# Scan convolutions as diagonal matmuls, 64-row steps in two row tiles, and doubled buffers, in a four-stage image kernel

## The reference

```
L0: channel attention: q,k,v = 1x1 convs; softmax over 64 channels; per image
L1: deformable 3x3 conv: offsets and mask = conv3x3(x); bilinear samples of x
    at 9 taps x mask; sum_k w_dcn[:, :, k] @ sample_k; batch norm; relu
L2: spatial attention: softmax(q^T k / 8) over 256 pixels; x + proj(attn @ v)
L3: y = depthwise3x3(ln2d(x));  o = sum over 4 directions of
    conv1d_5(y) * sigmoid(G_d y + g_b);  x = x + fuse(o)
    z = ff1(ln2d(x)); a, g = split(z); x + ff2(a * sigmoid(g))
```

## Time and profile before

| What | Value |
|---|---|
| median of the runs | 418.3 us (414.33 to 418.74) |
| span of the profiled execution | 416.3 us; its own run time is not listed apart, and it lies inside the runs |
| PE busy | 355.3 us (85%), 2060 matmul records |
| DVE busy | 286.1 us (69%) |
| ACT busy | 205.2 us (49%) |
| POOL busy | 107.6 us (26%) |
| chain that ended last | PE 52%, DVE 29%, issue 9%, ACT 6% |

### The profile page before, as it was taken

The page is one execution under the profiler, slowest core; times in us unless marked ns, Lnnn a source line. Parts: engine busy times, 40 slices in busy tenths (PEclk is TensorE's granted clock), DMA queues, the critical chain, the costliest instruction groups (busy, mean ns, idle before and its releaser), DMA issues.

```text
span 416.3 us, 6350 instructions
## 1 busy us (share of the span) xinstructions
PE 355.3 (85%) x2060; PEld 192.6 (46%) x2060; DVE 286.1 (69%) x623; ACT 205.2 (49%) x463; POOL 107.6 (26%) x178
## 2 busy tenths in 40 slices
PE   3759989998899989999899989999899988944613
PEld 2643545645455553645464554555464434324301
DVE  2226535595965878496978697596858698877681
ACT  1163365367416672477537652576337653543512
POOL 0130220140413231330424140422223141142241
PEclk9979999999869996899999986999689999997655
DMA  7000000000000000000000000000000000000000
GB/s 236 14 0 2 14 2 2 13 2 0 2 1 2 1 28 0 2 1 25 0 0 0 27 0 0 0 0 25 0 0 0 13 1 0 2 13 0 0 13 13
DMA packets 3042, 4.66 MB, mean 11 GB/s; under 512 B 336, under 2 KB 2768, under 8 KB 2896
## 3 DMA queue, kind: packets, MB, share of 16 engines
q1 hardware_dynamic: 3024, 4.43, 3.3%
HBM read 3.38 MB, written 1.05 MB: 11 GB/s over the span
## 4 chain that ended last, share of the span: by engine, by line
PE 52%; DVE 29%; issue 9%; ACT 6%; POOL 1%; DMA 1%; DVEq 0%; ACTq 0%; SPq 0%; POOLq 0%
PE ps_cv L497 13%; DVE sb_acc L992 10%; DVE sb_wt L933 5%; DVE sb_dw_acc L978 5%; PE ps_yb L481 5%; PE ps_ma L421 5%; PE ps_mb L568 4%; PE ps_mb L542 3%; PE ps_xb L478 3%; PE ps_mb L528 3%; PE ps_wx L465 2%; PE ps_mc L590 2%; ACT sb_xe L717 2%; PE ps_ma L412 2%; PE ps_ma L450 2%
## 5 line engine op out<-in xcount | busy, mean ns | idle before, releaser
L933 DVE TENSOR_TENSOR sb_wt<-ps_yb,sb_xe 128x512 f32<-128x512 f32 x144 | 97.2, 685 | 65.4 <-ACT sb_xe L717 49.2
L497 PE MATMUL ps_cv<-sb_wt,sb_w_x 128*64 128x256 f32 x576 | 100.0, 428 | 0.0
L481 PE MATMUL ps_yb<-sb_hats,sb_sel 128*128 128x512 f16 x144 | 57.6, 409 | 3.9 <-DVE sb_wt L933 3.7
L497 PEld LDWEIGHTS ps_cv<-sb_wt,sb_w_x 128*64 128x64 f32 x576 | 29.8, 141 | 55.3 <-issue 49.8
L992 DVE SCALAR_TENSOR_TENSOR sb_acc<-sb_y_pad,sb_par,sb_acc 128x256 f32<-128x256 f32 x96 | 52.1, 596 | 2.5 <-ACT sb_acc L788 2.4
L717 ACT ACTIVATE sb_xe<-ps_xb 128x512 f32<-128x512 f32 x72 | 43.0, 597 | 9.4 <-PE ps_xb L478 9.4
L1115 POOL TENSOR_TENSOR sb_acc<-sb_acc,sb_g_tmp 128x256 f32<-128x256 f32 x32 | 24.9, 779 | 63.2 <-ACT sb_acc L788 59.6
L978 DVE SCALAR_TENSOR_TENSOR sb_dw_acc<-sb_z_pad,sb_par,sb_dw_acc 128x256 f32<-128x256 f32 x56 | 36.7, 704 | 3.2 <-ACT sb_dw_acc L773 3.1
L465 PE MATMUL ps_wx<-sb_par,sb_x 128*128 128x256 f32 (+1 forms) x144 | 36.6, 376 | 0.4 <-ACT sb_w_x L708 0.4
L1075 POOL TENSOR_TENSOR sb_dist<-sb_pos,sb_par 128x1152 f32<-128x1152 f32 (+1 forms) x8 | 16.7, 2089 | 71.4 <-DVE sb_pos L886 71.4
L743 ACT ACTIVATE sb_b_exp<-ps_mb,sb_b_neg 128x256 f32<-128x256 f32 x28 | 13.0, 470 | 41.7 <-DVE sb_b_neg L943 41.7
(11 more groups left out here) (172 smaller groups left out, 547.4 us busy)
## 6 DMA issues: line engine op xcount, KB each, us to landing
sb_par<-in_par SPq DMA_DIRECT2D x1, 1339.5 KB, 8.5
sb_x_in<-in_x SPq DMA_DIRECT2D x8, 128.0 KB, 2.1
out_y<-sb_y_out SPq DMA_DIRECT2D x8, 128.0 KB, 1.7
sb_par<-in_par SPq DMA_DIRECT2D x1, 397.0 KB, 4.6
sb_sel<-in_sel SPq DMA_DIRECT2D x1, 224.0 KB, 4.7
sb_par<-in_par SPq DMA_DIRECT2D x1, 192.0 KB, 2.7
sb_par<-in_par SPq DMA_DIRECT2D x1, 128.0 KB, 2.2
```

Of the source, the lines that this page charges most:

```text
L481: nc.tensor.matmul(yb[h][:, :], sel_sb[:, P * (3 + 2 * odd + h):P * (4 + 2 * odd + h)], hats[:, g, :], start=True, stop=True).then_inc(ev( ...
L497: mm = nc.tensor.matmul(cv[C * b:C * (b + 1), 0:PIX], w_x[:, h, k, C * b:C * (b + 1)], wt[k % 2][h][:, PIX * b:PIX * (b + 1)], start=(s == ...
L933: nc.vector.tensor_tensor(wt[k % 2][h][:, :], yb[h][:, :], xe[k % 2][:, :], ALU.mult)\
```

## The change

- The four scan convolutions leave ACT, DVE and POOL. They become 20 fp32 matmuls with diagonal weights, two directions (128 output partitions) by two images, 5 taps each, in a new two-bank PSUM tensor `pair`. They read 64 rows each, the images in two row tiles. ACT evicts them (two of 512), one DVE operation of 1024 multiplies with the gates, and fuse sums the directions (4 matmuls).
- Gates, logits, ff1 and w_x become such 64-row steps too. The xb and yb matmuls read 32 rows, in different row groups.
- The exponentials are normalised on DVE and transposed in transpose mode, in place of the matmuls with diagonals.
- The w_x copies fall from five to three, hats, w_x and x3 have two buffers, the loop is written out and its register waits are gone. The plain copy of x1 moves to POOL. The constants to be loaded grow by 362 columns (185 KB), in the late transfer.
- PLAN is new: dist at POOL slot 8 (10 before), abs at ACT slot 9 (10 before), hat_y and dw0 at slot 11 (12 before), gate at 15, scan at 16. The product with the gates is at DVE's slot 0 of the next iteration.

```diff
+WX = ((0, 4), (4, 8), (8, 9))
...
-           14: ["wx3"], 15: ["tr0", "gate0"], 16: ["tr1", "ff2", "gate1"], 17: ["tr2"]},
...
+           10: ["a.wx0"], 12: ["a.wx1"], 13: ["a.wx2"], 15: ["b.gate", "a.tr0"], 16: ["b.scan", "a.tr1"],
+           17: ["a.tr2"]},
...
-        hats = sb("hats", [P, GROUPS, 2 * PIX], F16)
-        w_x = sb("w_x", [P, HALVES, TAPS, P])
+        hats = [sb(f"hats{i}", [P, GROUPS, 2 * PIX], F16) for i in range(2)]
+        w_x = [sb(f"w_x{i}", [P, 2, HALVES, TAPS, C]) for i in range(2)]
...
+        pair = bank("pair", 2)
...
-        def schedule(eng, iteration):
-            iteration(0, True, False, False, False)
-            iteration(1, True, True, False, False)
-            iteration(2, True, True, True, False)
-            iteration(3, True, True, True, True)
-            with eng.Fori(4, PAIRS) as n:
-                iteration(n, True, True, True, True)
-            iteration(PAIRS, False, True, True, True)
...
+        def run(engine, steps, main, last_a, begin):
+            for n in range(PAIRS + 1):
+                begin(n)
+                walk(engine, steps, main, last_a, n)
...
                     for h in range(HALVES):
-                        mm = nc.tensor.matmul(bank_wx(c, n)[:, 2 * P * h:2 * P * h + k], x1[:, P * h:P * (h + 1)],
-                                              par_sb[:, a:a + k], start=True, stop=True)
+                        for b in range(2):
+                            r = slice(C * b, C * (b + 1))
+                            mm = nc.tensor.matmul(pair[:, 512 * b + PIX * h:512 * b + PIX * h + k],
+                                                  x1[r, P * h:P * (h + 1)],
+                                                  par_sb[r, a:a + k], start=True, stop=True)
...
+                y = slice(2 * SLOT * odd, 2 * SLOT * odd + SLOT)
+                xx = slice(2 * SLOT * odd + SLOT, 2 * SLOT * (odd + 1))
...
-                    nc.tensor.matmul(xb[:, :], sel_sb[:, P * (1 + odd):P * (2 + odd)], hats[:, g, :],
+                    nc.tensor.matmul(xb[:, :], sel_sb[xx, P:2 * P], hats[n % 2][xx, g, :],
...
-                nc.tensor.matmul(yb[h][:, :], sel_sb[:, P * (3 + 2 * odd + h):P * (4 + 2 * odd + h)], hats[:, g, :],
+                nc.tensor.matmul(yb[h], sel_sb[y, P * (2 + h):P * (3 + h)], hats[n % 2][y, g, :],
...
+                for h in range(HALVES):
+                    for b in range(2):
+                        r = slice(C * b, C * (b + 1))
+                        mm = nc.tensor.matmul(bk[:, 512 * b + PIX * h:512 * b + PIX * (h + 1)],
+                                              q2[r, P * h:P * (h + 1)], k2[r, :], start=True, stop=True)
...
-                            mm = nc.tensor.matmul(bk[:, PIX * j + P * h:PIX * j + P * (h + 1)],
-                                                  b_exp[b][:, h, P * j:P * (j + 1)], b_dia[b][:, h, :],
-                                                  start=True, stop=True)
+                            mm = nc.tensor.transpose(bk[:, PIX * j + P * h:PIX * j + P * (h + 1)],
+                                                     b_nrm[:, b, h, P * j:P * (j + 1)], ident)
...
+            def gate(n):
+                bk = pair_of("gate", n)
+                pe.wait_ge(ev("y_ok"), n)
+                wait_past(pe, ev("wx_ok"), chunk(min(n + 2, PAIRS), len(WX) - 1))
+                wait_past(pe, ev("ff_act"), n - 1)
+                for d in range(2):
+                    a = AT["gate_w"][0] + P * d
+                    for b in range(2):
+                        r = slice(C * b, C * (b + 1))
+                        mm = nc.tensor.matmul(bk[:, 512 * b + PIX * d:512 * b + PIX * (d + 1)], par_sb[r, a:a + P],
+                                              y_pad[r, 2:2 + H, 2:2 + W], start=True, stop=True)
+                mm.then_inc(ev("gate_mm"), 1)
+            def scan(n):
+                bk = pair_of("scan", n)
+                if not is_last(n):
+                    pe.wait_ge(ev("gate_ok"), n)
+                for d in range(2):
+                    for j in range(KS):
+                        a = AT["scan_w"][0] + P * (KS * d + j)
+                        for b in range(2):
+                            r = slice(C * b, C * (b + 1))
+                            rows = y_pad[r, 2:2 + H, j:j + W] if d == 0 else y_pad[r, j:j + H, 2:2 + W]
+                            mm = nc.tensor.matmul(bk[:, 512 * b + PIX * d:512 * b + PIX * (d + 1)], par_sb[r, a:a + P],
+                                                  rows, start=(j == 0), stop=(j == KS - 1))
+                mm.then_inc(ev("scan_mm"), 1)
...
-                nc.tensor.matmul(bk[:, 0:PIX], fuse_h[:, :], o_sum[:, :], start=True, stop=True)\
+                for d in range(2):
+                    for b in range(2):
+                        mm = nc.tensor.matmul(bk[C * b:C * (b + 1), 0:PIX], fuse_h[:, :], prod[:, d, b, :],
+                                              start=(d == 0), stop=(d == 1))
...
+                for j in range(2):
+                    for b in range(2):
+                        r = slice(C * b, C * (b + 1))
+                        mm = nc.tensor.matmul(bk[:, 512 * b + PIX * j:512 * b + PIX * (j + 1)],
+                                              par_sb[r, a + HID * j:a + HID * (j + 1)], z2[r, :], start=True, stop=True)
...
-            def scan(j):
-                def step(n, nb):
-                    for d in range(3):
-                        dve.wait_ge(ev(f"scan{d}"), scan_count(n, j - 1))
-                        nc.vector.scalar_tensor_tensor(out=image(acc[d][j % 2][:, :]), in0=window(d, j),
-                                                       scalar=col("scan_w", d * KS + j),
-                                                       in1=image(acc[d][(j - 1) % 2][:, :]), op0=ALU.mult, op1=ALU.add)\
-                            .then_inc(ev(f"scan{d}"), 1)
-                return step
...
+            def prod_step(n):
+                dve.wait_ge(ev("gate_ok"), n)
+                dve.wait_ge(ev("scan_ok"), n)
+                nc.vector.scalar_tensor_tensor(out=prod[:, :, :, :].rearrange("p d b q -> p (d b q)"),
+                                               in0=gates[:, :, :, :].rearrange("p d b q -> p (d b q)"), scalar=1.0,
+                                               in1=conv[:, :, :, :].rearrange("p d b q -> p (d b q)"),
+                                               op0=ALU.add, op1=ALU.mult).then_inc(ev("prod_ok"), 1)
...
+            def x1_step(n):
+                pool.wait_ge(ev("x1_pad_ok"), n)
+                nc.gpsimd.tensor_copy(image(x1[:, :]), x1_pad[:, 1:1 + H, 1:1 + W]).then_inc(ev("x1_ok"), 1)
...
-            def scan3(n, nb):
-                d = 3
-                settle(pool)
-                pool.wait_ge(ev("y_ok"), n)
-                a = d * KS
-                for j in range(1, KS):
-                    nc.gpsimd.tensor_scalar(image(g_tmp[j % 2][:, :]), y_pad[:, j:j + H, 2:2 + W], col("scan_w", a + j),
-                                            0.0, ALU.mult, ALU.add).then_inc(ev("term"), 1)
-                    pool.wait_ge(ev("term"), n * (KS - 1) - (KS - 1) + j)
-                    pool.wait_ge(ev(f"scan{d}"), scan_count(n, j - 1))
-                    nc.gpsimd.tensor_tensor(acc[d][j % 2][:, :], acc[d][(j - 1) % 2][:, :], g_tmp[j % 2][:, :], ALU.add)\
-                        .then_inc(ev(f"scan{d}"), 1)
```

631 lines of the change are left out of this document (266 added, 365 removed), and 17 rows, old and new, of tables (PLAN, PLAN_END).

## The result

The changed kernel takes 463.2, 463.0 and 468.9 us in three runs; a fourth of 491.6 us, at a granted clock of 0.738, counts in the median of 466.0 and not in the ratio. The kernel before takes 418.35. The ratio is 1.113, with a 95% interval of 1.104 to 1.122. The forecast was 423.5 with a range of 387 to 449: slower was the likeliest of the three outcomes at 0.45, and the size was far too small: 5 us against 48.

The account below looks back on a forecast made before the run. It took the chain to y_pad (33.5 us) and on to x2 (13.6) to bound a period of 47; 60.5 + 44.5 + 235 + 35.5 + 46 = 421.5, plus 2.0, gave 423.5 us, range 387 to 449.

Parts of the forecast that it names:

- the clock term: Full iterations: a clock dip falls into slots that then have slack, so nothing was added for it.
- The rival on the clock: Behind PE's waits: clock falls in every iteration, 4.6 us more in five or six iterations, 446 to 451 us; chance 0.15.
- The chain behind y_pad: From y_pad through gates, copies and scans to x2: 13.6 us at full clock, 5.9 before.
- xb beside yb: Selector matmuls on PE: running side by side saves 9 × 0.22, −2.0 us of PE's list per full iteration.
- The last main: Last main, without transpositions behind the scans: 34.2 + 1.3 = 35.5 us.
- The iteration without c: First to second x2: 38.9 − 3 + 7.7 = 43.6 us, taken as 44.5.
- PE's list: PE's work per full iteration: −2.8 us in sum, some 37.6 long, up to 41.2 with drains for mode changes.
- what PE waits for at full clock is not in these slots: Slots 0 to 5: the relief of DVE, POOL and ACT lies there and was costed at nothing.
- The relief of DVE and POOL: DVE loses scan operations: 27 us busy per iteration expected, no bound; relief costed at nothing in slots 0 to 5.
- PE's list as the bound: Full iterations: y_pad at 28 behind x2, PE's list of 41 sets the period, time 384.5 us; chance 0.13.
- the shorter chain: Chain to y_pad: dw2 pair falls out of the split's overlap, −2.1, period 45 or 44, 405 to 412 us; chance 0.20.
- that rival: Row-tiled steps on PE: tiles do not run beside each other, scans take 8.8 us, time about 465; chance 0.05.

Follow-up runs that it names:

- the filler: Matmuls that nothing reads in PE's waits: of the changed kernel, 453.0 us; for the 17 us, one at each of two slot 2 waits, kernel before, 400.6 us.
- s3: Changed kernel with one tap of five in the scans, 4 matmuls in place of 20, so less work: 435.5 us (1.048).
- the rearranged versions: Changed kernel with scans behind the next pair's first xb and yb, 439.4 us; also with 128-row selectors and four filler matmuls in slot 13, 422.5 us.
- s7: Changed kernel with the xb and yb selector matmuls reading 128 rows again: 456.5 us (1.097).
- s8: Changed kernel with the scans behind the first xb and yb of the next pair, and 128-row selectors: 425.3 us (1.025).
- s4: Changed kernel with the scans image by image, so neighbouring records use the same rows and cannot overlap: 539.3 us (1.298).
- t1: Changed kernel with the exponentials transposed by ordinary fp32 matmuls with the identity in place of transpose mode: 485.8 us (1.169).
- b1: Kernel before with one part of the change alone, xb and yb reading their 32 rows: 427.3 us (1.028).
- f3: Kernel before with 32-row selectors and two filler matmuls at each of two waits in slot 2: 409.1 us (0.985).
- s1: Changed kernel with the scans moved from slot 16 to slot 1 of the next iteration, product, fuse and ff1 later: 459.0 us (1.102).

## Why the prediction was wrong

The span was 39.9 us above the forecast's 421.5: first x2 +4.2 (64.7 for 60.5), the iteration without c +5.4, five full ones +22.0 (257.0 for 235), last main +8.8, tail −0.5.

- **The step that failed** is the clock term: "A dip like that of the earlier trace rows falls into slots that then have slack, so I add nothing for it." The lower level fell into the two places that have no slack: behind x2, where b starts, and behind y_pad. Per full iteration it cost 51.4 − 47.25 = 4.15, as the filler showed in the two iterations that it brought to full clock; that is nearly all of the 4.4 by which the period of 47 was too low. y_pad came 36.5 behind x2 for 33.5 (33.4 at full clock), and x2 14.9 behind y_pad for 13.6 (13.8). The rival on the clock had this mechanism and its size, 4.6 in each iteration, at a chance of 0.15; its 446 to 451 was still short by the other items here. The slack that the step counted on was PE's 9 us of idle time (7.8 measured); but PE's waits are no slack where the step behind the wait is the next link of the chain.
- **The chain behind y_pad was right**, in its order and its length at full clock. The scans cost their whole 4.6 (s3: 3.6 for four fifths of them). Their position behind the gates' copies and ahead of tr1 cost the larger part of what the rearranged versions won back (27 of 44 us, from 466.0 by way of 439.4 to 422.5).
- **What I had in no term**: that narrow matmuls hold the clock down. I counted xb beside yb as −2.0 of PE's list. It gave −0.45 of PE's busy time in a warm iteration and 0.1 of the period, and it cost 6.8 us before the first x2 in the kernel before. In the changed kernel undoing it gained some 7 to 10 us, nearly all of it in the last main; in the full iterations it showed only with the scans last. That the width itself holds the clock is the likeliest reading of the two kernels that differ in nothing else; as the first x2 of the changed kernel does not move with it, the condition stays open.
- **The last main** was walked wrongly. I took 34.2 + 1.3, as if the gates and scans there were nearly free without the transpositions. The chain y_pad, gates, scans, x2 stands in it too (11.6 for 4.1 before). At full clock the last main is 37.7 (s7, with 128-row selectors), and in the changed kernel 44.3, as its clock was 0.77.
- **The iteration without c** was put at 44.5 and took 49.9. y_pad came 34.1 behind x2 and not the 30.7 that the forecast's −3 makes of 33.7, and x2 15.9 behind y_pad and not 12.9. Its clock was 0.87; no run splits these 6.3 us into clock and list.
- **PE's list** at full clock was 37.6 by the forecast. Without the −2.0 for the narrow selectors, that is 39.6. In s8's iteration at full clock PE is busy 40.14 with 128-row selectors, against 40.45 before: the row-tiled steps and the shorter transpositions just pay for the scans, no more.
- **One reading was wrong**: "what PE waits for at full clock is not in these slots", of slots 0 to 5. In the fast iteration of the kernel before, PE waits 0.34, 0.71 and 0.77 in slots 0 to 2, and that is 1.8 of its 2.0 idle us. The two longer waits are the ones that the filler closed, for 17 us.
- **The relief of DVE and POOL** (27.0 of 51.4 us busy, as forecast) bought nothing that shows in the period. The rivals that needed it, PE's list as the bound and the shorter chain, are out: in a full iteration y_pad was not before 33.4 behind x2 in any version of the changed kernel.
- **Row tiles overlap**, as the earlier trace rows said. A pair took 0.23, so that rival is out, and s4 shows its price as 10.1 us per iteration.

For the full iterations the two items, 4.15 of clock and 0.25 of chain, make up the 22.0. What stays open: why t1 is slower by more than its list, and what part of the first x2's 64.7 is the clock (the level is low from 20 to 37 us, 26 to 33 before) and what part the copies of the first pair.

## What to carry to other kernels

Work moved onto an engine inside a cycle costs its whole length unless it lands in a wait of that engine; ask which wait it fills, and who is queued behind it. Packing TensorE in row tiles shortens its list only if the freed time isn't given back in the clock: look at the granted clock of a stretch before and after, not at the busy share. And where an iteration has two speeds at the same work, look for the waits ahead of the slow stretch; one cheap matmul in each of two waits made the kernel 3.6% faster here, while the rebuilt kernel was 11% slower, and 1.6% slower in its best version.

## What the runs showed of the hardware

- TensorE stayed at the lower level for over 16 us of unbroken work when a good part of it was 32-row matmuls (0.50 in 34 to 50 us), where the same work in 128 rows was at 1.00 (b1; f3 shows the same from 28 to 48 us). In the changed kernel, though, 32-row matmuls did not keep it down: 1.00 from 38 to 64 us (but 0.50 from 28 to 48 in s1).
- 40 fp32 records of 64 rows and 256 columns took 4.6 us as neighbouring pairs in two row halves at 1.00, and 14.3 us as two runs of 20 in one half each, most of it at the lower level.
- Two waits of 0.71 and 0.77 us stood ahead of a dip of the clock that cost 4.6 us in four of the five full iterations; in the fifth they stood there without a dip. With 0.48 us of each filled there was none.
- Four fp32 transpositions of 128 by 128 took 0.59 us in transpose mode and 1.09 as matmuls with the identity.
